# The residual sum r formed by an accumulating transfer on arrival, in place of GpSimd's additions

## The chip, the cores and the metric

The kernel runs on one core of one Trainium2 chip. The metric is the device time of one execution in microseconds (us). TensorE, VectorE, ScalarE, GpSimd and SyncE are called PE, DVE, ACT, POOL and SP in the profile.

## The reference

x has 8 batches of 512 tokens and 2048 features, all in fp32. With W, b the base weight and bias and A, B the low-rank factors that a batch's id selects, the reference computes

```
h    = x @ W.T + b + (x @ A.T) @ B.T
q    = h @ Wq.T
s    = router scores of q against 512 slots (through Wr), plus log_rel
w    = softmax over the 8 best slots of (q . keys / 8 + log_rel)
aux  = (w @ values) @ Wvd.T @ Wvu.T
u    = clip(0.5 * log1p(var(h)) / mean(log1p(var(h))) + 2.5 * sigmoid(gelu(h @ Wu1.T + bu1) @ Wu2.T), 0, 5)
gate = sigmoid(0.5 * clip((u - 0.5) / 1.5, 0, 1) - 1), 0 where under 0.05
out  = x + h + gate * aux
```

The change concerns one sum of the last line, r = x + h. The product gate * aux is added to it at the end.

## The kernel before

Everything lies transposed: a tile is 128 features by 512 tokens in fp32 (256 KB), so a batch is KT = 16 tiles and all eight are 128 tiles. fp32 products are made of three matmuls of a high and a low part.

The first stage (to about 1340 us of the profile) computes h by seven block products for each pair of batches and stores it in DRAM (h_dram). It does not touch r.

The second stage is a loop of STEPS = 128 steps, one tile of h each, batch c = step // 16, k = step % 16. Each engine runs its own copy of the loop in its own fixed order, and semaphores tie them. In a step, SP loads a tile of h into hraw (load_h, a ring of four, four steps ahead); ACT and DVE split it into its high and low part (h_hi, h_lo, two steps ahead, ring h_sp of four); PE does twelve matmuls for Wu1 (u_pass, L1954 to L1956) and two for Wq (L1971, L1972). In the first 16 steps batch 7's query is made too, early, out of the tiles of h that come for r: ACT and DVE split them (h7_hi, h7_lo, ring of two) and PE multiplies them (query7_pass, L1979 and L1980). From step 16 on the work on the batch before (gelu, scores, choice of 8, softmax, transposes, z) is woven into the steps.

r needs a second walk over the tiles, in another order. Its index n runs with the steps. The first NPRE = 32 are batches 7 and 6; ACT stores these sums to r_dram (store_pre), and SP reads them back as r67 (load_last, 512 KB for each k) from step 115 on, for the end. The other 96 are batches 0 to 5: at step 32 + a, PE makes three matmuls of aux for tile a (aux_pass, L2074 to L2076, into one bank), and DVE adds the bank to r's tile and writes o_st (add_out, L1741), which ACT stores (store_out). PE's next aux_pass waits for that addition (out_ready).

For each n, SP loads two tiles in load_r: x into r_x and h into r_h, each a ring of four, two steps ahead. POOL adds them in place into r_h (L891, semaphore r_ready); nothing else is on POOL in these steps but a few memsets. SP's load of x waits for r_ready of n - 4 and its load of h for the store (r_dram, n < 36) or for DVE's add_out (later) of n - 4. What stands behind load_r in SP's queue is the next load_h, and from step 115 load_last.

After step 127 a tail finishes batches 6 and 7 from r67; seven aux banks are copied by ACT into the places of r_x and r_h (evacuated) and added by POOL.

Of the kernel before, what the change touches and what calls it, by code (L numbers as in the profile page):

```python
# [7 lines left out]
KT = D // P  # L8
NB = 8
# [41 lines left out]
def bass_adaln_ffn(  # L51
# [25 lines left out]
    ADD, SUB, MULT = ALU.add, ALU.subtract, ALU.mult  # L77
# [9 lines left out]
    with ctx:  # L87
        def sem(name):
            return ctx.enter_context(nc.semaphore(name))

        def wait(eng, semaphore, value):
            if value > 0:
                eng.wait_ge(semaphore, value)
# [216 lines left out]
        gate_step = sem("gate_step")  # L310
        mstep = sem("mstep")
        ln_ready = sem("ln_ready")
        mean_done = sem("mean_done")
        qb_ready = sem("qb_ready")
        qt_ready = sem("qt_ready")
        qf_ready = sem("qf_ready")
# [13 lines left out]
        zh_ready = sem("zh_ready")  # L330
        zl_ready = sem("zl_ready")
        aux_done = sem("aux_done")
        r_ready = sem("r_ready")
        out_ready = sem("out_ready")
        step_out = [sem(f"step_out{i}") for i in range(4)]
        r67_in = [sem(f"r67_in{i}") for i in range(4)]
# [219 lines left out]
        def evacuated(j):  # L556
            return r_x[:, j, :] if j < 4 else r_h[:, j - 4, :]

        block = ctx.enter_context(nc.Block())


        @block.sync
        def _(sp):
# [104 lines left out]
                sp.dma_start(hraw[:, m % 4, :], h_dram[c, k]).then_inc(hr_in[m % 4], 16)  # L668

            def load_r(n):  # L670
                if n < NPRE:
                    b, o = NB - 1 - n // KT, n % KT
                else:
                    b, o = (n - NPRE) // KT, n % KT
                if n == 0:

                    sp.wait_ge(main_done, TILES - 1)
                    stored(sp, h_index(NPAIR - 1, M5, HT - 1) + 1)
                if n == KT:
                    stored(sp, 4 * HT * NPAIR)  # L680
                wait(sp, r_ready, n - 3)
                sp.dma_start(r_x[:, n % 4, :], x[b, o]).then_inc(rxh_in[n % 4], 16)
                if 4 <= n < NPRE + 4:
                    sp.wait_ge(step_out[n % 4], 16 * (n // 4))
                elif n >= NPRE + 4:
                    sp.wait_ge(out_ready, n - 4 - NPRE + 1)
                sp.dma_start(r_h[:, n % 4, :], h_dram[b, o]).then_inc(rxh_in[n % 4], 16)

            def load_last(k):
                if k < KT - 1:  # L690
# [93 lines left out]
                    sp.wait_ge(a7_out, 16 * TT)  # L784
                sp.dma_start(att[:, t, :], a7_dram[t]).then_inc(a7_in, 16)

            load_r(0)
            load_r(1)
            for step in range(STEPS):
                if step + 4 < STEPS:  # L790
                    load_h(step + 4)
                if step + 2 < STEPS:
                    load_r(step + 2)
                if step >= (NB - 1) * KT + 3:
                    load_last(step - (NB - 1) * KT - 3)
                if step - (NB - 1) * KT in (7, 10, 13):
                    load_a7((step - (NB - 1) * KT - 7) // 3)
# [25 lines left out]
        def _(pool):  # L823
# [61 lines left out]

            pool.wait_ge(qb_ready, 1)
            for n in range(STEPS):
                pool.wait_ge(rxh_in[n % 4], 32 * (n // 4 + 1))
                if n < KT:
                    pool.wait_ge(h7l_ready, n + 1)  # L890
                pool.tensor_tensor(r_h[:, n % 4, :], r_h[:, n % 4, :], r_x[:, n % 4, :], ADD).then_inc(r_ready, 1)  # L891
                if n == KT + 2:
                    pool.wait_ge(h7_used, KT)
                    pool.wait_ge(r_ready, n + 1)
                    pool.memset(qb7[BOT:P, :].bitcast(f32), 1.0).then_inc(qb_ready, 1)
                    pool.wait_ge(qb_ready, 2)
            pool.wait_ge(r_ready, STEPS)
            pool.wait_ge(wgt_ready, len(SEQ) + TT // 2)
            for j in range(KT - BY_DVE):
                o = BY_DVE + j  # L900
# [6 lines left out]
        def _(act):  # L907
# [267 lines left out]
                    .then_inc(gelu_ready, 1)  # L1175

            def h7_hi(n):
                act.wait_ge(rxh_in[n % 4], 32 * (n // 4 + 1))
                wait(act, h7_used, n - 1)
                to_hi(h7_sp[n % 2][:, 0, :], r_h[:, n % 4, :]).then_inc(h7h_ready, 1)  # L1180

            def query_copy(b):
                if b == EARLY:
# [66 lines left out]
                    .then_inc(zh_ready, 1)  # L1250

            def store_pre(n):
                act.wait_ge(r_ready, n + 1)
                act.dma_start(r_dram[n % KT, :, 1 - n // KT, :], r_h[:, n % 4, :]).then_inc(step_out[n % 4], 16)

            def store_out(a):
                act.wait_ge(out_ready, a + 1)
                act.dma_start(out[a // KT, a % KT], o_st[:, a % 4, :]).then_inc(step_out[a % 4], 16)

            def store_step(step):  # L1260
                if step < NPRE:
                    store_pre(step)
                else:
                    store_out(step - NPRE)

            def evacuate(j):
                a = NAUX + BY_DVE + j
                act.wait_ge(aux_done, aux_count(a))
                if j == 0:
                    act.wait_ge(r_ready, STEPS)  # L1270
                    act.wait_ge(out_ready, NAUX)
                act.activation(evacuated(j), aux_place(a)[:], ACT.Copy).then_inc(ev_ready, 1)

            for step in range(STEPS):
                c, k = step // KT, step % KT
                b = c - 1
                if step + 2 < STEPS:
                    h_hi(step + 2)
                if c == 0:
                    h7_hi(k)  # L1280
                if c == 0 and k in (3, 5):
                    split_wvu_hi((k - 3) // 2)
                if c == 0 and k in (5, 7):
                    copy_stats(NB - 2 + (k - 5) // 2)
                if c == 0 and k == 9:
                    act.wait_ge(mstep, 4)
                    act.activation(norm_t[:], var_t[:], ACT.Ln, bias=1.0).then_inc(ln_ready, 1)
                if c >= 1:
                    if k == 0:
                        for m in range(FT):  # L1290
                            gelu(b, m)
                        query_copy(b)
                    if k == 1:
                        query_hi(b)
                    if k == 2:
                        sigmoid_learned(b)
                    if k in MASK_AT:
                        exp_tile(POS[b, MASK_AT[k]])
                    if k == 1 and early_tile(c - 1) is not None:
                        exp_tile(POS[EARLY, early_tile(c - 1)])  # L1300
                    if k == 4 and early_tile(c - 1) is not None:
                        store_a7(early_tile(c - 1))
                    if k == 3:
                        sigmoid_gate(b)
                    if k in TURN_AT:
                        wt_hi(b * TT + TURN_AT[k])
                    if k in Z_AT:
                        z_hi(b, Z_AT[k])
                    if k == 4 and c == 1:
                        query_copy(EARLY)  # L1310
                    if k == 6 and c == 1:
                        query_hi(EARLY)
                if step > 0:
                    store_step(step - 1)

            b, i = NB - 1, (NB - 1) * TT
            for m in range(FT):
                gelu(b, m)
            evacuate(0)
            evacuate(1)  # L1320
            store_step(STEPS - 1)
            sigmoid_learned(b)
            sigmoid_gate(b)
            evacuate(2)
# [15 lines left out]
        def _(dve):  # L1340
# [250 lines left out]

            def h7_lo(n):
                dve.wait_ge(h7h_ready, n + 1)
                lo(h7_sp[n % 2][:, 1, :], r_h[:, n % 4, :], h7_sp[n % 2][:, 0, :]).then_inc(h7l_ready, 1)

            def query_sum(b):
                ps = aux_bank if b == EARLY else q_ps
# [82 lines left out]
                dve.tensor_reduce(rowsum[:], norm_t[:].rearrange("p b t -> p (b t)"), AX.X, ADD).then_inc(mstep, 1)  # L1680

            def mean_of_logs():
                dve.wait_ge(mean_done, 1)
                dve.tensor_scalar(inv_t[:], mean_ps, 1.0 / NTOK, 1e-6, MULT, ADD).then_inc(mstep, 1)
                dve.wait_ge(mstep, 6)
                dve.reciprocal(inv_t[:], inv_t[:]).then_inc(mstep, 1)
                dve.wait_ge(mstep, 7)
                dve.tensor_scalar(norm_t[:], norm_t[:], inv_t[:], 0.5, MULT, MULT).then_inc(mstep, 1)
# [47 lines left out]

            def add_out(a):
                dve.wait_ge(aux_done, a + 1)
                dve.wait_ge(r_ready, NPRE + a + 1)
                dve.wait_ge(step_out[a % 4], 16 * ((NPRE + a) // 4))  # L1740
                dve.tensor_tensor(o_st[:, a % 4, :], aux_bank[:], r_h[:, a % 4, :], ADD).then_inc(out_ready, 1)  # L1741

            def add_last6(o):
                a = NAUX + o
# [88 lines left out]
        def _(pe):  # L1833
# [244 lines left out]
            for step in range(STEPS):  # L2078
                c, k = step // KT, step % KT
                b = c - 1  # L2080
                if c >= 1:
                    if k in TURN_AT:
                        turn_pass(b * TT + TURN_AT[k])
                    if k in Z_AT:
                        z_pass(b, Z_AT[k])
                    if k == 2:
                        learned_pass(b)
                    if k in SCORE_AT:
                        score_pass(POS[b, SCORE_AT[k]])
                    if k == KT - 2 and early_tile(c) is not None:  # L2090
                        score_pass(POS[EARLY, early_tile(c)])
                elif k == 4:
                    stats_pass(NB - 2)
                elif k == 6:
                    stats_pass(NB - 1)
                elif k == 13:
                    pe.wait_ge(mstep, 5)
                    pe.matmul(mean_ps, ones[:], rowsum[:], start=True, stop=True).then_inc(mean_done, 1)
                if 0 <= step - Q7_LAG < KT:
                    query7_pass(step - Q7_LAG)  # L2100
                u_pass(step)
# [81 lines left out]
```

## Time and profile before

| | |
|---|---|
| median of 3 runs | 1915.87 us (1915.84 to 1920.31) |
| profiled execution, its own time | 1916.47 us |
| its span, first to last instruction | 1913.9 us |
| PE busy | 1898.0 us, 99% |
| DVE, ACT, POOL busy | 67%, 37%, 21% |
| DMA traffic | 412 MB, mean 215 GB/s |

The execution's own time is 2.6 us above its span; that part lies outside the trace. A row of a group gives its line, engine, operation, output <- input, shape and count, then busy time in all, mean ns of one, and the idle time of the engine before them with what ended it. Matmul durations overlap: one is listed at 390 ns, but the next starts some 227 ns after it.

### The profile page before, as it was taken

What the parts mean: (1) busy time and instruction counts of PE and PEld (TensorE: products, weight loads), DVE (VectorE), ACT (ScalarE), POOL (GpSimd) and SP (SyncE); (2) the same over time, 40 slices, a digit from 0 to 9 for tenths busy, and PEclk for the clock granted to TensorE, in tenths of its full rate; (3) what the DMA queues carried; (4) which work ended last, traced back from release to release, by engine and by line L of the source; (5) the groups of instructions that cost most, each with busy time, mean ns of one, the idle gap of its engine ahead of it and who ended that gap; (6) DMA issues with size and microseconds to landing.
All of it is one profiled execution on the core that took longest, in us unless ns stands there. A gap on an engine that the chain in (4) does not pass through costs nothing.

```text
span 1913.9 us, 24642 instructions
## 1 busy us (share of the span) xinstructions
PE 1898.0 (99%) x8480; PEld 1550.8 (81%) x8480; DVE 1286.4 (67%) x1686; ACT 714.2 (37%) x1133; POOL 397.4 (21%) x275
## 2 busy tenths in 40 slices
PE   8999999999999999999999999999999999999998
PEld 6888888888888888888888888877888888888887
DVE  5786788565468746447864745777776677677676
ACT  4332344333234333224433333445444234333333
POOL 2210232020023202002310100220443323322332
PEclk9999999999999999999999999999999999999999
DMA  7856877451456745146664425666988777777797
GB/s 279 305 180 216 288 250 230 153 181 60 149 201 232 241 144 179 55 157 216 230 219 146 165 91 192 233 202 226 319 276 286 232 239 243 233 237 247 228 363 295
DMA packets 195633, 412.35 MB, mean 215 GB/s; under 512 B 26740, under 2 KB 28276, under 8 KB 195382
## 3 DMA queue, kind: packets, MB, share of 16 engines
q1 hardware_dynamic: 150006, 321.64, 51.2%
q10 hardware_dynamic: 45504, 89.15, 12.2%
q8 instruction: 68, 1.11, 0.2%
q14 instruction: 55, 0.45, 0.1%
HBM read 313.17 MB, written 97.52 MB: 215 GB/s over the span
## 4 chain that ended last, share of the span: by engine, by line
PE 95%; DVE 3%; ACT 1%; issue 1%; DMA 0%; ACTq 0%; DVEq 0%; SPq 0%
PE bank L1915 21%; PE bank L1916 21%; PE bank L1917 21%; PE bank L1954 6%; PE bank L1955 6%; PE bank L1956 6%; PE bank L1858 2%; PE bank L2074 2%; PE bank L1859 2%; PE bank L2076 1%; PE bank L2075 1%; PE bank L1846 1%; PE bank L1972 1%; PE bank L1971 1%; PE bank L2039 1%
## 5 line engine op out<-in xcount | busy, mean ns | idle before, releaser
L1915 PE MATMUL bank<-xop,wsp 128*128 128x512 f32 x1792 | 701.8, 392 | 6.0 <-DVE wsp L1342 6.0
L1916 PE MATMUL bank<-xop,wsp 128*128 128x512 f32 x1792 | 700.3, 391 | 0.0
L1917 PE MATMUL bank<-xop,wsp 128*128 128x512 f32 x1792 | 699.2, 390 | 0.0
L1915 PEld LDWEIGHTS bank<-xop,wsp 128*128 128x128 f32 x1792 | 337.4, 188 | 85.4 <-DVE wsp L1342 6.4
L1917 PEld LDWEIGHTS bank<-xop,wsp 128*128 128x128 f32 x1792 | 337.1, 188 | 71.8
L1916 PEld LDWEIGHTS bank<-xop,wsp 128*128 128x128 f32 x1792 | 337.6, 188 | 70.6
L909 ACT ACTIVATE wsp<-wraw 128x1024 fp32r<-128x1024 f32 x184 | 195.0, 1060 | 495.7 <-PE bank L1917 487.8
L1342 DVE TENSOR_TENSOR wsp<-wraw,wsp 128x1024 fp32r<-128x1024 f32 x184 | 234.8, 1276 | 154.9 <-ACT wsp L909 154.1
L891 POOL TENSOR_TENSOR r_h<-r_h,r_x 128x512 f32<-128x512 f32 x128 | 175.3, 1370 | 358.3 <-DMA r_h<-h_dram 322.9
L1954 PE MATMUL bank<-h_sp,wu 128*128 128x512 f32 x512 | 200.5, 392 | 1.4 <-DVE stage L1428 1.4
L1955 PE MATMUL bank<-h_sp,wu 128*128 128x512 f32 x512 | 199.8, 390 | 0.0
L1956 PE MATMUL bank<-h_sp,wu 128*128 128x512 f32 x512 | 199.5, 390 | 0.0
L1442 DVE TENSOR_TENSOR sums<-sums,stage 128x1024 f32<-128x1024 f32 x120 | 162.7, 1356 | 0.7 <-ACT stage L994 0.4
L854 POOL TENSOR_TENSOR xraw<-xraw 128x512 f32<-128x512 f32 x32 | 52.2, 1631 | 500.9 <-DMA xraw<-in_x 500.9
L1342 DVE TENSOR_TENSOR xop<-xraw,xop 128x512 fp32r<-128x512 f32 x184 | 153.0, 861 | 3.6 <-ACT xop L909 3.0
L1342 DVE TENSOR_TENSOR h_sp<-hraw,h_sp 128x512 fp32r<-128x512 f32 x128 | 102.8, 803 | 36.4 <-ACT h_sp L909 35.2
L1954 PEld LDWEIGHTS bank<-h_sp,wu 128*128 128x128 f32 x512 | 96.2, 188 | 22.4 <-DVE stage L1428 1.8
L1741 DVE TENSOR_TENSOR o_st<-bank,r_h 128x512 f32<-128x512 f32 x96 | 66.0, 688 | 70.9 <-PE bank L2076 70.6
L1956 PEld LDWEIGHTS bank<-h_sp,wu 128*128 128x128 f32 x512 | 96.1, 188 | 20.7
L1955 PEld LDWEIGHTS bank<-h_sp,wu 128*128 128x128 f32 x512 | 96.2, 188 | 19.6
L909 ACT ACTIVATE xop<-xraw 128x512 fp32r<-128x512 f32 x184 | 107.7, 617 | 5.7 <-DMA xraw<-in_x 5.0
L909 ACT ACTIVATE h_sp<-hraw 128x512 fp32r<-128x512 f32 x128 | 80.1, 627 | 74.3 <-DVE o_st L1741 59.3
(187 smaller groups left out, 1953.7 us busy)
## 6 DMA issues: line engine op xcount, KB each, us to landing
xraw<-in_x SPq DMA_DIRECT2D x248, 256.0 KB, 4.2
wraw<-in_w SPq DMA_DIRECT2D x123, 512.0 KB, 3.8
wraw<-t_dram SPq DMA_DIRECT2D x80, 512.0 KB, 3.6
h_dram<-stage ACTq DMA_DIRECT2D x128, 256.0 KB, 2.7
hraw<-h_dram SPq DMA_DIRECT2D x128, 256.0 KB, 4.1
r_x<-in_x SPq DMA_DIRECT2D x128, 256.0 KB, 4.4
r_h<-h_dram SPq DMA_DIRECT2D x128, 256.0 KB, 3.6
out<-o_st ACTq DMA_DIRECT2D x96, 256.0 KB, 3.9
```

The source lines that it names most:

```text
L854: pool.tensor_tensor(tile, tile, x_raw("b21", p, k), ADD).then_inc(s1_ready, 1)
L891: pool.tensor_tensor(r_h[:, n % 4, :], r_h[:, n % 4, :], r_x[:, n % 4, :], ADD).then_inc(r_ready, 1)
L909: return act.activation(dst, src, ACT.Copy)
L1342: return dve.tensor_tensor(dst, src, hi.bitcast(f32), SUB)
L1442: dve.tensor_tensor(into, into, stage[:, n % NST, :, :], ADD).then_inc(sum_ready, 1)
L1741: dve.tensor_tensor(o_st[:, a % 4, :], aux_bank[:], r_h[:, a % 4, :], ADD).then_inc(out_ready, 1)
L1915: pe.matmul(ps, wsp[:, slot, 0, f], x_hi(i), start=(k == 0), stop=False)
L1916: pe.matmul(ps, wsp[:, slot, 0, f], x_lo(i), start=False, stop=False)
L1917: last = pe.matmul(ps, wsp[:, slot, 1, f], x_hi(i), start=False, stop=(k == HT - 1))
L1954: pe.matmul(u_ps[m][:], wu[k][:, 0, f], h_sp[step % 4][:, 0, :], start=(k == 0), stop=False)
L1955: pe.matmul(u_ps[m][:], wu[k][:, 0, f], h_sp[step % 4][:, 1, :], start=False, stop=False)
L1956: last = pe.matmul(u_ps[m][:], wu[k][:, 1, f], h_sp[step % 4][:, 0, :], start=False, stop=(k == KT - 1))
```

## The change

r is formed by the transfers themselves. SP loads only h, into r_t(n), a place of a ring of eight (the four of r_x and the four of r_h together). When it has landed, and in the first 16 steps also h7_lo has read it, POOL issues a transfer from x in DRAM onto the same tile with accum_op=ADD, so that x is added on arrival. It completes on one of two semaphores r_in (even and odd n), and POOL first waits for the completion of n - 2, so that at most two accumulations are under way. SP's loads run four steps ahead and wait for the user of n - 8. The load order in a step stays load_h, then load_r. ACT stores a pre-sum one step later (store_pre(step - 2) at the end of a step) and waits for r_in of it and for the store of n - 4; store_out stays in its place. add_out waits for r_in of its tile. The semaphore mean_done is replaced by a further count of stats_done. The arithmetic of everything else is unchanged.

```diff
+        def r_t(n):
+            return (r_x if n % 8 < 4 else r_h)[:, n % 4, :]
+        def wait_r(eng, n):
+            eng.wait_ge(r_in[n % 2], 16 * (n // 2 + 1))
...
             def load_r(n):
...
-                wait(sp, r_ready, n - 3)
-                sp.dma_start(r_x[:, n % 4, :], x[b, o]).then_inc(rxh_in[n % 4], 16)
-                if 4 <= n < NPRE + 4:
-                    sp.wait_ge(step_out[n % 4], 16 * (n // 4))
-                elif n >= NPRE + 4:
-                    sp.wait_ge(out_ready, n - 4 - NPRE + 1)
-                sp.dma_start(r_h[:, n % 4, :], h_dram[b, o]).then_inc(rxh_in[n % 4], 16)
+                wait(sp, rxh_in[n % 4], 16 * (n // 4))
+                if n >= 8 and n - 8 < NPRE:
+                    sp.wait_ge(step_out[n % 4], 16 * ((n - 8) // 4 + 1))
+                elif n >= 8:
+                    sp.wait_ge(out_ready, n - 8 - NPRE + 1)
+                sp.dma_start(r_t(n), h_dram[b, o]).then_inc(rxh_in[n % 4], 16)
...
-            load_r(0)
-            load_r(1)
+            for n in range(4):
+                load_r(n)
             for step in range(STEPS):
                 if step + 4 < STEPS:
                     load_h(step + 4)
-                if step + 2 < STEPS:
-                    load_r(step + 2)
+                if step + 4 < STEPS:
+                    load_r(step + 4)
...
             for n in range(STEPS):
-                pool.wait_ge(rxh_in[n % 4], 32 * (n // 4 + 1))
+                b, o = r_source(n)
+                pool.wait_ge(rxh_in[n % 4], 16 * (n // 4 + 1))
                 if n < KT:
                     pool.wait_ge(h7l_ready, n + 1)
-                pool.tensor_tensor(r_h[:, n % 4, :], r_h[:, n % 4, :], r_x[:, n % 4, :], ADD).then_inc(r_ready, 1)
+                if n >= 2:
+                    wait_r(pool, n - 2)
+                pool.dma_start(r_t(n), x[b, o], accum_op=ADD).then_inc(r_in[n % 2], 16)
...
             def store_pre(n):
-                act.wait_ge(r_ready, n + 1)
-                act.dma_start(r_dram[n % KT, :, 1 - n // KT, :], r_h[:, n % 4, :]).then_inc(step_out[n % 4], 16)
+                wait_r(act, n)
+                wait(act, step_out[n % 4], 16 * (n // 4))
+                act.dma_start(r_dram[n % KT, :, 1 - n // KT, :], r_t(n)).then_inc(step_out[n % 4], 16)
...
-                if step > 0:
-                    store_step(step - 1)
+                if 0 <= step - 2 < NPRE:
+                    store_pre(step - 2)
+                if step > NPRE:
+                    store_out(step - 1 - NPRE)
...
             def add_out(a):
                 dve.wait_ge(aux_done, a + 1)
-                dve.wait_ge(r_ready, NPRE + a + 1)
+                wait_r(dve, NPRE + a)
```

## Rows read from the trace of the kernel before

**Rows 1.** The page: busy time by engine, and the chain that ended last.
```profile
PE 1898.0 (99%) x8480; PEld 1550.8 (81%) x8480; DVE 1286.4 (67%) x1686; ACT 714.2 (37%) x1133; POOL 397.4 (21%) x275
...
PE 95%; DVE 3%; ACT 1%; issue 1%; DMA 0%; ACTq 0%; DVEq 0%; SPq 0%
```

**Rows 2.** Busy time by stretch; last columns: granted clock, DMA share, GB/s.
```profile
1340.00:1460.00 120.00, 118.59 (x543) 97.81 (x542) 81.89 (x135) 53.96 (x100) 49.93 (x35) 1.00 0.86 295
1460.00:1840.00 380.00, 378.64 (x1764) 313.66 (x1764) 267.30 (x522) 133.68 (x248) 115.24 (x86) 1.00 0.74 244
1840.00:1880.00 40.00, 40.00 (x195) 33.44 (x194) 24.43 (x46) 11.77 (x22) 10.67 (x8) 1.00 1.00 386
```

**Rows 3.** PE's waits, 1340 to 1880 us: in total, times, longest.
```profile
PE bank L2074 <- DVE o_st L1741: 1.4, 2, 1.0
PE bank L2003 <- DVE qa L1342: 0.8, 1, 0.8
PE bank L1979 <- DVE h_sp L1342: 0.5, 1, 0.5
```

**Rows 4.** Groups by line and shape, 1340 to 1880 us.
```profile
L891 POOL TENSOR_TENSOR r_h<-r_h,r_x 128x512 f32<-128x512 f32 x128 | 175.3, 1370 | 358.3 <-DMA r_h<-h_dram 322.9 <-DVE h_sp L1342 35.4
L1342 DVE TENSOR_TENSOR h_sp<-hraw,h_sp 128x512 fp32r<-128x512 f32 x126 | 101.4, 805 | 36.4 <-ACT h_sp L909 35.2
```

**Rows 5.** Tile acc, durations min/median/max; then timelines of DVE and POOL.
```profile
L1696 DVE TENSOR_SCALAR acc<-gact,wu_sb x8: 476/480/1449, 1396.8 to 1879.3; 128x512 f32<-128x512 f32 x8
...
1396.76 1.45 DVE L1696 TENSOR_SCALAR acc<-gact,wu_sb 128x512 f32<-128x512 f32 x1 [1.23 <-ACT gact L1174]
...
1395.07 4.29 POOL L891 TENSOR_TENSOR r_h<-r_h,r_x 128x512 f32<-128x512 f32 x3 [2.33 <-DVE h_sp L1342]
```

**Rows 6.** Tile r_h: durations ns, first and last start us.
```profile
L1741 DVE TENSOR_TENSOR o_st<-bank,r_h x96: 675/691/693, 1465.1 to 1882.3; 128x512 f32<-128x512 f32 x96
L1254 ACTq DMA_DIRECT2D r_dram<-r_h x32: 326/326/362, 1346.5 to 1459.0; - x32
L909 ACT ACTIVATE h_sp<-r_h x16: 615/632/633, 1342.1 to 1393.6; 128x512 fp32r<-128x512 f32 x16
```

**Rows 7.** DMA issues, 1340 to 1460 us: count, KB, median us to landing.
```profile
r_h<-h_dram SPq DMA_DIRECT2D x33, 256.0 KB, 4.4
hraw<-h_dram SPq DMA_DIRECT2D x33, 256.0 KB, 4.7
r_x<-in_x SPq DMA_DIRECT2D x32, 256.0 KB, 4.8
```

**Rows 8.** DMA issues, 1460 to 1840 us.
```profile
hraw<-h_dram SPq DMA_DIRECT2D x87, 256.0 KB, 4.0
...
r<-r_dram SPq DMA_DIRECT2D x4, 512.0 KB, 5.8
```

**Rows 9.** Timelines of ACT, then DVE: one period of the first sixteen steps.
```profile
1386.30 0.63 ACT L909 ACTIVATE h_sp<-r_h 128x512 fp32r<-128x512 f32 x1 [2.71 <-PE bank L1980]
1386.33 0.33 ACTq L1254 DMA_DIRECT2D r_dram<-r_h  x1
...
1389.94 0.63 ACT L909 ACTIVATE h_sp<-r_h 128x512 fp32r<-128x512 f32 x1 [2.49 <-PE bank L1980]
...
1386.96 0.69 DVE L1342 TENSOR_TENSOR h_sp<-r_h,h_sp 128x512 fp32r<-128x512 f32 x1 [2.57 <-ACT h_sp L909]
```

**Rows 10.** SP's waits, 1340 to 1880 us.
```profile
SPq L687 <- DVE o_st L1741: 268.5, 91, 5.2
SPq L687 <- DMA r_dram<-r_h: 72.5, 25, 5.9
```

**Rows 11.** Two stretches of 6 us, columns as in rows 2.
```profile
1848.00:1854.00 6.00, 6.00 (x34) 5.19 (x33) 4.31 (x9) 0.99 (x2) 1.29 (x1) 1.00 1.05 410
1878.00:1884.00 6.00, 5.69 (x30) 4.58 (x29) 3.94 (x6) 3.83 (x7) 0.00 (x0) 1.00 0.41 136
```

**Rows 12.** DMA issues, 1840 to 1880 us.
```profile
hraw<-h_dram SPq DMA_DIRECT2D x4, 256.0 KB, 8.7
```

More of the change, by code:

```diff
@@ L312, in bass_adaln_ffn @@
         ln_ready = sem("ln_ready")
-        mean_done = sem("mean_done")
         qb_ready = sem("qb_ready")
@@ L332, in bass_adaln_ffn @@
         aux_done = sem("aux_done")
-        r_ready = sem("r_ready")
+        r_in = [sem(f"r_in{i}") for i in range(2)]
         out_ready = sem("out_ready")
@@ L557, in evacuated, with r_source @@
             return r_x[:, j, :] if j < 4 else r_h[:, j - 4, :]
+        def r_t(n):
+            return (r_x if n % 8 < 4 else r_h)[:, n % 4, :]
+        def r_source(n):
+            return (NB - 1 - n // KT, n % KT) if n < NPRE else ((n - NPRE) // KT, n % KT)
+        def wait_r(eng, n):
+            eng.wait_ge(r_in[n % 2], 16 * (n // 2 + 1))
         block = ctx.enter_context(nc.Block())
@@ L670, in load_r @@
             def load_r(n):
[L671 to L674, printed above, removed]
+                b, o = r_source(n)
                 if n == 0:
@@ L887, in _ @@
             for n in range(STEPS):
-                pool.wait_ge(rxh_in[n % 4], 32 * (n // 4 + 1))
+                b, o = r_source(n)
+                pool.wait_ge(rxh_in[n % 4], 16 * (n // 4 + 1))
                 if n < KT:
                     pool.wait_ge(h7l_ready, n + 1)
-                pool.tensor_tensor(r_h[:, n % 4, :], r_h[:, n % 4, :], r_x[:, n % 4, :], ADD).then_inc(r_ready, 1)
+                if n >= 2:
+                    wait_r(pool, n - 2)
+                pool.dma_start(r_t(n), x[b, o], accum_op=ADD).then_inc(r_in[n % 2], 16)
                 if n == KT + 2:
                     pool.wait_ge(h7_used, KT)
-                    pool.wait_ge(r_ready, n + 1)
                     pool.memset(qb7[BOT:P, :].bitcast(f32), 1.0).then_inc(qb_ready, 1)
                     pool.wait_ge(qb_ready, 2)
-            pool.wait_ge(r_ready, STEPS)
+            wait_r(pool, STEPS - 2)
+            wait_r(pool, STEPS - 1)
             pool.wait_ge(wgt_ready, len(SEQ) + TT // 2)
@@ L1177, in h7_hi @@
             def h7_hi(n):
-                act.wait_ge(rxh_in[n % 4], 32 * (n // 4 + 1))
+                act.wait_ge(rxh_in[n % 4], 16 * (n // 4 + 1))
                 wait(act, h7_used, n - 1)
-                to_hi(h7_sp[n % 2][:, 0, :], r_h[:, n % 4, :]).then_inc(h7h_ready, 1)
+                to_hi(h7_sp[n % 2][:, 0, :], r_t(n)).then_inc(h7h_ready, 1)
             def query_copy(b):
@@ L1258, in store_out @@
                 act.dma_start(out[a // KT, a % KT], o_st[:, a % 4, :]).then_inc(step_out[a % 4], 16)
[L1260 to L1264, printed above, removed]
             def evacuate(j):
@@ L1269, in evacuate @@
                 if j == 0:
-                    act.wait_ge(r_ready, STEPS)
+                    wait_r(act, STEPS - 2)
+                    wait_r(act, STEPS - 1)
                     act.wait_ge(out_ready, NAUX)
@@ L1320, in _ @@
             evacuate(1)
-            store_step(STEPS - 1)
+            store_out(NAUX - 1)
             sigmoid_learned(b)
@@ L1593, in h7_lo @@
                 dve.wait_ge(h7h_ready, n + 1)
-                lo(h7_sp[n % 2][:, 1, :], r_h[:, n % 4, :], h7_sp[n % 2][:, 0, :]).then_inc(h7l_ready, 1)
+                lo(h7_sp[n % 2][:, 1, :], r_t(n), h7_sp[n % 2][:, 0, :]).then_inc(h7l_ready, 1)
             def query_sum(b):
@@ L1682, in mean_of_logs @@
             def mean_of_logs():
-                dve.wait_ge(mean_done, 1)
+                dve.wait_ge(stats_done, NB + 1)
                 dve.tensor_scalar(inv_t[:], mean_ps, 1.0 / NTOK, 1e-6, MULT, ADD).then_inc(mstep, 1)
@@ L1738, in add_out @@
                 dve.wait_ge(aux_done, a + 1)
-                dve.wait_ge(r_ready, NPRE + a + 1)
+                wait_r(dve, NPRE + a)
                 dve.wait_ge(step_out[a % 4], 16 * ((NPRE + a) // 4))
-                dve.tensor_tensor(o_st[:, a % 4, :], aux_bank[:], r_h[:, a % 4, :], ADD).then_inc(out_ready, 1)
+                dve.tensor_tensor(o_st[:, a % 4, :], aux_bank[:], r_t(NPRE + a), ADD).then_inc(out_ready, 1)
             def add_last6(o):
@@ L2097, in _ @@
                     pe.wait_ge(mstep, 5)
-                    pe.matmul(mean_ps, ones[:], rowsum[:], start=True, stop=True).then_inc(mean_done, 1)
+                    pe.matmul(mean_ps, ones[:], rowsum[:], start=True, stop=True).then_inc(stats_done, 1)
                 if 0 <= step - Q7_LAG < KT:
```

## Prediction

> **What bounds the kernel now.** I read the page first: PE is busy in 99% of the span and 95% of the chain that ended last is PE's [rows 1]. The change acts only between 1340 and 1880 us, so I read the stretches next. PE lacks 1.4 us of 120 and 1.4 of 380, and nothing of the last 40, at a granted clock of 1.00, which is the level of 2.4 GHz [rows 2]. PE's own waits there name DVE each time, 2.7 us in all [rows 3]; none names POOL or a transfer. DMA is the second resource: a share of 0.86 at 295 GB/s in the first 32 steps, 0.74 at 244 GB/s in the long middle, 1.00 at 386 GB/s at the end [rows 2]. POOL's additions take 175.3 us, but it idles 358.3 us before them [rows 4]: it is no bound. So nearly nothing is to be won, and the question is whether the new transfer takes so much of the DMA engines, or so long, that PE begins to wait.
>
> **What is removed.** 128 additions of 1370 ns on POOL [rows 4]. None lies on PE's chain, so their 175 us are worth nothing by themselves. Their effect on DVE is worth something: while POOL ran three additions in a row from 1395.07, DVE's multiplication of acc took 1.45 us, against a median of 0.48 over its eight occurrences [rows 5]. That slow patch lies just ahead of the place where PE waits 0.8 us for qa, and the 0.5 us for h_sp (L1979) also falls in the first 16 steps, where DVE splits two tiles a step; I count both as won, 1.3 us. Of the 1.4 us for o_st [rows 3], which comes once aux is under way, I count 0.2, because one addition on POOL in 4.39 us seldom meets that chain. Gain 1.5 us; bounds 0 and 2.7 us (all of these waits).
>
> **What is moved.** SP's load of h for r goes four steps ahead, with a ring of eight. Today SP's largest wait there is for the place of r_h, 268.5 us behind DVE's add_out and 72.5 us behind the store [rows 10], and the next load_h stands behind it. With n - 8 in place of n - 4 most of this goes, and SP is then held by load_h's own condition. hraw lands in a median of 4.7 and 4.0 us [rows 7, 8] and no wait of PE names it, so this is cover, not gain: zero. The single load in place of two saves SP some 0.4 us an issue; zero also. store_pre one step later and mean_done folded into stats_done: zero, as the events awaited are the same or older; the price of store_pre's new wait is below.
>
> **What is added.** 128 accumulating transfers that GpSimd issues, of which the trace shows none. Two costs have to be bounded.
>
> First, their share of the DMA engines. An accumulation reads x and the tile and writes the tile. Below, it costs what the load of x costs now (nothing added). Above, I take two plain copies: one more tile, 262 KB, per step. The pace: 32 stores from 1346.5 to 1459.0 us make 3.63 us a step, 96 add_outs from 1465.1 to 1882.3 make 4.39 [rows 6]. One more tile is 72 GB/s early (295 becomes 367) and 60 GB/s in the middle (244 becomes 304). The engines have shown 410 GB/s [rows 11]. So even the upper value fits, at 0.90 and 0.74 of that. I take the upper value. In the last 40 us DMA is full already; about seven accumulations fall there, 1.8 MB, 4.5 us of work at 410 GB/s. It is absorbed: at 1878 to 1884 the share is down to 0.41 [rows 11], and the last tiles of r67 are used in the tail only; hraw lands late there, 8.7 us [rows 12], but is fetched some three steps (13 us) ahead of its split. Zero.
>
> The Trainium skill (Collectives: The Full Stack, The bandwidth ceiling) says that an add in the DMA engine costs no cycles itself but needs two source reads, and gives a ratio of 1.93. By it the added share would be 0.93 of a tile, 67 GB/s in place of my 72, and the sum is the same; no row here shows an accumulation.
>
> Second, their latency L, from issue to landing. Only two may be under way, so one is finished every L/2. For L below: x's plain landing of 4.8 us [rows 7] and ACT's issue of 0.33 [rows 6], 5.1 us. Above: two plain landings after each other, 4.8 + 4.4 [rows 7], and a GpSimd issue as long as the addition it replaces, 1.37 [rows 4]: 10.6 us. Nearest is the transfer that reads as much as an accumulation does, 512 KB, with 5.8 us [rows 8]. Scaled to the fuller first 32 steps by hraw's 4.7 to 4.0 it is 6.8, with an issue of 0.33 to 1.37 it is 7.1 to 8.2 us early and 6.1 to 7.2 later. I take 7.1, at the low end, as the reads of x and of the tile go on side by side in 16 engines.
>
> What L costs PE early: batch 7's tile is split by ACT at 1386.30, DVE has read it at 1387.65 and then the accumulation may start. ACT's new store stands two periods of 3.64 us later, at 1393.58 [rows 9], so 5.9 us of L are hidden. ACT idles 2.5 us a step there [rows 9], and it splits for PE two steps ahead, of which some 5 us are left after the two splits: PE waits only when the store is 7.5 us late. At L = 7.1 the pair's pace is 3.55 us, the store is 1.2 us late, and ACT's idle time takes it. But lag adds up: the first 16 steps take only 3.43 us each (15 intervals from 1342.1 to 1393.6 [rows 6]), and from the first store to the last it is 112.5 us. The last pre-sum lands 31 L/2 + L = 16.5 L after the first may start, and PE's limit is 112.5 + 5.9 + 7.5 = 125.9 us: L = 7.6 us. Later the limit is 2 x 4.39 = 8.8 us, with a lead of four steps on top. At 7.1 both hold: zero.
>
> Queued behind the waits: on ACT the splits of the next step; on POOL only the next accumulation; on SP (h for r waits for the store of n - 8) load_h. All three are covered as long as L is under the limit.
>
> **Sum.** 1.5 us less. Against the profiled execution 1916.47 becomes 1915.0; it lay 0.6 us above the median of 1915.87, so the median becomes 1914.4 us. 0.3% is 5.7 us, about what a measurement of this kernel can tell from no change, so this is "same".
>
> **Rivals.** (a) *Two at a time is too few.* From L = 7.6 us on PE waits for ACT's splits, and from 8.1 the net loss passes 5.7 us. At L = 9: early 16.5 x 9 - 125.9 = 23 us, later (4.5 - 4.39) x 96 = 10 us, in all +33, less 1.5: 1947 us. At the bound of 10.6 it is 49 + 87 us and 2050. For it: L's upper half; landings stretch to 8.7 us when the engines are full [rows 12]. Against: 410 GB/s is well above 367. It is the slower case that I hold likeliest, and store_pre's wait is its place.
>
> The Trainium skill (SBUF - State Buffer, SBUF: two separate sides) has a rule against this change: a transfer issued by GpSimd can stall because GpSimd writes its descriptors through a port that DVE's two-port operations lock. This would lengthen L; the trace shows only that POOL and DVE slow each other [rows 5], and no GpSimd transfer. In this kernel such operations are few and short (0.48 us), so it enters as part of rival (a).
>
> (b) *The DMA engines become the bound.* If an accumulation costs four plain copies in place of one, a step moves seven tiles, 1.83 MB, 4.48 us at 410 GB/s: +0.85 x 32 + 0.09 x 96 = 36 us, less 1.5: 1950 us. It decides from 2.6 copies on early ((410 - 295) x 3.63 / 262 = 1.6 tiles of room) and from 3.8 later. DMA's share would stand at 1.00 over the whole loop.
>
> (c) *PE gains more than its waits.* A gain over 5.7 us would need more than the 2.7 us of waits, so a change in the tail (1880 to 1913.9), where POOL's seven additions stay. 1909 us. Nothing speaks for it.
>
> (d) *It does not matter at all*, because the waits of [rows 3] are DVE's own chain and stay: 1915.9 us. It lies inside the likeliest case.
>
> **Chances.** Likeliest with (d), within 0.3%: 0.59. (a) 0.24, (b) 0.13, (c) 0.04. So faster 0.04, same 0.59, slower 0.37. The likeliest's own range is 1912 to 1921. For 8 in 10 the low end takes the gain's bound (1913.2) and a little for run spread, 1912; the high end takes (a) up to L = 9 (1947) and leaves out what lies above, most of (b) too: 1947.
>
> **What the profile after would show.** DVE's waits on PE's list fall from 2.7 us towards 1.2, and the 1.45 us multiplication returns to 0.48; if not, the gain is wrong. DMA's share in the first 32 steps is 0.95 to 1.00 and in the middle 0.8 to 0.95; if it stays at 0.74 an accumulation is cheap, if it is 1.00 everywhere (b) holds. Issue to landing of the accumulation under 7.6 us: if over 8.1, ACT's splits wait for r and PE for h_sp, and (a) holds. SP's wait behind add_out nearly vanishes.

## The result, and the profile after

The changed kernel takes 1920.59 us in the median of 20 runs, the kernel before 1917.86 us in 20 runs beside them: a ratio of 1.0013, 95% interval 1.0007 to 1.0019. It is slower by 0.13%, or 2.7 us. The size is inside the forecast's "same" (0.3%) and inside its range, but the sign is wrong: 1.5 us less was forecast, and the interval excludes no change. The profiled execution took 1921.71 us with a span of 1919.7 us, 5.8 us above the span before, a high draw, as that of before was a low one of its own runs.

The page of the changed kernel, as [rows 1]:

```profile
span 1919.7 us, 24772 instructions
...
PE 1900.7 (99%) x8480; PEld 1552.4 (81%) x8480; DVE 1253.1 (65%) x1686; ACT 713.8 (37%) x1133; POOL 333.5 (17%) x275
...
PE 92%; DMA 3%; DVE 2%; ACT 1%; issue 1%; SPq 0%; ACTq 0%; DVEq 0%; POOLq 0%
```

DMA has appeared on the chain that ended last, with 3%. Busy time by stretch, columns as in [rows 2]:

```profile
1340.00:1460.00 120.00, 115.36 (x511) 94.49 (x510) 68.24 (x130) 49.13 (x94) 29.92 (x35) 0.97 1.02 282
1460.00:1840.00 380.00, 379.02 (x1771) 314.40 (x1770) 249.00 (x517) 136.08 (x251) 76.07 (x88) 1.00 0.93 246
1840.00:1880.00 40.00, 40.00 (x191) 33.31 (x190) 25.59 (x52) 10.42 (x20) 6.05 (x7) 1.00 1.07 350
```

All that was lost is lost in the first 32 steps: PE lacks 4.6 us of 120 there, against 1.4 before, and the mean granted clock is 0.97. Later PE is as busy as before or busier. PE's waits around and after the join of the two stages, the larger ones, as [rows 3]:

```profile
PE bank L1960 <- ACT gact L1182: 3.6, 1, 3.6
PE bank L1960 <- DVE stage L1434: 1.1, 1, 1.1
PE bank L2080 <- DVE o_st L1747: 0.9, 1, 0.9
PE bank L1985 <- DVE h_sp L1348: 0.6, 1, 0.6
PE bank L1874 <- ACT stats L1008: 0.5, 1, 0.5
```

The wait for stage is not new: it lies in the first step of the second stage, and in the kernel before it is 1.4 us and ends at 1338.95, just ahead of where [rows 3] begin. The wait for qa is gone and that for o_st shorter (0.9 in place of 1.4 us), as forecast in kind; that for h_sp stays. New is a wait of 0.5 us for ACT's copy of the statistics, at 1360.49, and one of 3.6 us for the gelu of batch 0, at the first matmul of step 16. ACT's own timeline says why it was late:

```profile
1392.04 0.33 ACTq L1263 DMA_DIRECT2D r_dram<-r_x  x1
1392.47 0.63 ACT L917 ACTIVATE h_sp<-hraw 128x512 fp32r<-128x512 f32 x1 [4.32 <-DMA r_x<-in_x]
...
1394.55 0.33 ACTq L1263 DMA_DIRECT2D r_dram<-r_h  x1
...
1398.34 0.33 ACTq L1263 DMA_DIRECT2D r_dram<-r_h  x1
1398.77 0.63 ACT L917 ACTIVATE h_sp<-hraw 128x512 fp32r<-128x512 f32 x1 [2.64 <-DMA r_h<-in_x]
1399.42 1.28 ACT L1182 ACT_TABLE_LOAD   x1
1400.71 0.69 ACT L1182 ACTIVATE gact<-bank,bu_sb 128x512 f32<-128x512 f32 x1
```

The store at 1398.34 is that of n = 13, which stands in ACT's queue at the end of step 15. It was held until x had been added to that tile. Only then came the next split, the load of gelu's table and the gelu. PE had started its last matmul of step 15 at 1397.57, and up to there it had lost 0.5 us, the wait for the statistics: the first step begins 0.3 us and this one ends 0.9 us later than before. The chain that ended last goes through the accumulations here:

```profile
1378.39 6.06 DMA r_x<-in_x
1384.51 0.49 issue
1385.00 7.02 DMA r_x<-in_x
1392.09 0.49 issue
1392.58 5.75 DMA r_h<-in_x
1398.34 0.33 ACTq L1263
```

Three accumulations after one another in one of the two lanes (even n and odd n), each let in by the landing of n - 2 and 0.5 us later under way. It was so, within a microsecond, in both lanes from n = 5 to n = 15. GpSimd's issues of n = 3 and n = 13:

```profile
1355.84 0.86 POOL L899 DMA_DIRECT2D r_x<-in_x  x1 [1.52 <-DVE h_sp L1348]
...
1392.58 0.86 POOL L899 DMA_DIRECT2D r_h<-in_x  x1 [4.33 <-DMA r_x<-in_x]
```

Ten tiles in 36.7 us are 3.67 us per tile, 7.35 us a round. PE's own steps from 3 to 13 take 36.8 us in the kernel before, so r kept pace but could not catch up what it was late from the start on. The other part of the loss is the clock. Four-microsecond stretches, columns as above:

```profile
1396.00:1400.00 4.00, 1.96 (x9) 1.30 (x7) 1.51 (x3) 1.35 (x3) 0.86 (x1) 1.00 1.10 276
1400.00:1404.00 4.00, 2.45 (x6) 2.00 (x7) 2.37 (x5) 3.96 (x7) 0.86 (x1) 0.60 1.05 309
1404.00:1408.00 4.00, 4.00 (x12) 3.10 (x11) 3.68 (x6) 1.42 (x3) 0.86 (x1) 0.55 1.07 313
```

The granted clock fell to the level of 1.2 GHz at 1400.8, while PE still waited, and stayed there until 1407.6: 14 matmuls started 0.43 us apart in place of 0.23, another 2.8 us. With the waits of 3.6 and 0.5 that makes 6.9 us; less what went of the others (0.8 for qa, 0.5 for o_st, 0.3 for stage) it is 5.3 us. The spans differ by 5.8 us, and the second stage began 0.3 us later (its first matmul at 1336.38 in place of 1336.04), so 0.2 us are left.

DMA in the first 120 us of the loop, queues and issues, as [rows 7]:

```profile
q1 hardware_dynamic: 9478, 17.26, 42.0%
q0 software_dynamic: 4738, 8.64, 42.0%
q10 hardware_dynamic: 4320, 7.87, 17.6%
...
hraw<-h_dram SPq DMA_DIRECT2D x32, 256.0 KB, 6.0
r_x<-in_x POOLq DMA_DIRECT2D x18, 256.0 KB, 6.1
...
r_h<-in_x POOLq DMA_DIRECT2D x16, 256.0 KB, 6.5
```

q0 is GpSimd's. It takes the same share as SP's q1 with half of the packets of the same mean size: 0.420 x 16 x 120 us / 4738 = 170 ns a packet against 85.

### The profile page after: what moved, and what is told of

It is laid out like the page before. It is cut to its first block, busy times and chain, and to the rows that moved or that the text cites. A ratio compares the mean times of both kernels' runs of the same rounds, so it can differ in the third digit from the quotient of the medians.

```text
span 1919.7 us, 24772 instructions
## 1 busy us (share of the span) xinstructions
PE 1900.7 (99%) x8480; PEld 1552.4 (81%) x8480; DVE 1253.1 (65%) x1686; ACT 713.8 (37%) x1133; POOL 333.5 (17%) x275
## 4 chain that ended last, share of the span: by engine, by line
PE 92%; DMA 3%; DVE 2%; ACT 1%; issue 1%; SPq 0%; ACTq 0%; DVEq 0%; POOLq 0%
PE bank L1921 20%; PE bank L1922 20%; PE bank L1923 20%; PE bank L1960 5%; PE bank L1961 5%; PE bank L1962 5%; PE bank L1864 2%; PE bank L2080 2%; PE bank L1865 2%; PE bank L2082 1%; PE bank L2081 1%; PE bank L1852 1%; PE bank L2045 1%; PE bank L1978 1%; PE bank L1977 1%; DMA r_x<-in_x 1%
## 5 line engine op out<-in xcount | busy, mean ns | idle before, releaser
L1448 DVE TENSOR_TENSOR sums<-sums,stage 128x1024 f32<-128x1024 f32 x120 | 158.7, 1322 | 0.7 <-ACT stage L1002 0.4
L1348 DVE TENSOR_TENSOR h_sp<-hraw,h_sp 128x512 fp32r<-128x512 f32 x128 | 88.2, 689 | 67.9 <-ACT h_sp L917 66.2
L853 POOL TENSOR_TENSOR xraw<-xraw,v_t 128x512 f32<-128x512 f32 x32 | 54.6, 1717 | 243.6 <-DMA xraw<-in_x 243.6
L1002 ACT ACTIVATE stage<-stage 128x512 f32<-128x512 f32 x128 | 79.3, 619 | 40.4 <-DVE stage L1434 37.6
```

What stands on the lines that cost most here:

```text
L853: pool.tensor_tensor(tile, tile, v_t[:, k, :], ADD).then_inc(s2_ready, 1)
L1002: act.activation(stage[:, n % NST, 1, :], stage[:, n % NST, 0, :], ACT.Square).then_inc(sq_ready, 1)
L1348: return dve.tensor_tensor(dst, src, hi.bitcast(f32), SUB)
L1448: dve.tensor_tensor(into, into, stage[:, n % NST, :, :], ADD).then_inc(sum_ready, 1)
```

## The experiments

Each was timed against the kernel before on the same chip. Theory A is ACT's place in the queue; theory B, that the DMA engines are full.

**The changed kernel again.**

> The changed kernel again, unaltered, as the base of this set. Theory A (ACT's place): in the first 16 steps two accumulations at a time finish one per 3.5 us or slower against 3.43 us a step, ACT waits for r_in in store_pre, comes late to the four gelus of step 16, PE waits some 3 to 4 us for them and then runs some 6 us at the lower clock: +2 to +5 us over before, with the wait for gelu in the trace in most executions. Theory B (the DMA engines are full in the first 32 steps): the same time, but the lost time would be spread, without one single wait.

1920.88 us, ratio 1.0010 (1.0001 to 1.0018). Its profile has the same single long wait, 3.6 us for gact, and the same pace of 3.67 us per tile from n = 3 to 13. The clock was at 1.2 GHz for half as long behind it, 3.4 us (1404.1 to 1407.5), which is 8 matmuls and 1.6 us. The wait of theory A repeats; the price of the clock varies.

**Four accumulations under way.**

```diff
-            eng.wait_ge(r_in[n % 2], 16 * (n // 2 + 1))
+            eng.wait_ge(r_in[n % 4], 16 * (n // 4 + 1))
...
-                if n >= 2:
-                    wait_r(pool, n - 2)
+                if n >= 4:
+                    wait_r(pool, n - 4)
```

> Four accumulations may be under way in place of two; nothing else changes (two freed semaphores come from the r67 loads sharing v_in). Theory A: the pace of two at a time is gone, ACT is in time for gelu, PE's wait for gelu falls to 0 and the clock stays 1.00: 3 to 6 us less than the changed kernel, level with before or 1 us under it. Theory B: the engines were full with two; four under way only lengthen each landing (from 6 to 10 us or more), ACT waits as long and the time stays at +2 to +5 us.

1916.07 us, ratio 0.9991 (0.9982 to 1.0000): 2.2 per thousand (4.2 us) less than the changed kernel's 1.0013, as A says; against its repeat in this set it is 1.9 per thousand. But the wait for gelu did not go to zero. PE's wait and the landings from 1340 to 1460 us:

```profile
PE bank L1959 <- ACT gact L1181: 2.1, 1, 2.1
...
hraw<-h_dram SPq DMA_DIRECT2D x33, 256.0 KB, 7.0
r_x<-in_x POOLq DMA_DIRECT2D x19, 256.0 KB, 7.3
```

With more under way each lands later (7.3 against 6.1 us) and so does h itself. ACT's last wait ahead of the gelus is for such a load of h, with the store of n = 13 issued at 1395.05 inside it:

```profile
1395.59 0.63 ACT L916 ACTIVATE h_sp<-hraw 128x512 fp32r<-128x512 f32 x1 [2.22 <-DMA hraw<-h_dram]
```

B holds for that part: the engines are full (a share of 1.03), and ACT stays near the edge.

**The stores issued by GpSimd.**

```diff
+                if 0 <= n - 2 < NPRE:
+                    wait(pool, r_st[(n - 2) % 4], 16 * ((n - 2) // 4))
+                    pool.dma_start(r_dram[(n - 2) % KT, :, 1 - (n - 2) // KT, :], r_t(n - 2)).then_inc(r_st[(n - 2) % 4], 16)
...
-                if 0 <= step - 2 < NPRE:
-                    store_pre(step - 2)
```

> The 32 stores of the pre-sums are issued by GpSimd, after its own wait for r_in of n - 2, so that ACT waits for no accumulation; two at a time stay, and GpSimd gets a second issue per step. Theory A: PE's wait for gelu is gone although the accumulations are as slow, the time is level with before (+-1 us). Theory B: the time stays at +2 to +5 us, as the DMA work is the same.

1924.22 us, ratio 1.0032 (1.0021 to 1.0043): slower, which neither theory gave. The wait for gelu shrank to 0.9 us as A says, but a new one came:

```profile
PE bank L2076 <- DVE o_st L1743: 6.5, 2, 5.7
```

It is at the first aux products. PE's second ones wait for DVE's first add_out, and DVE stood still before that:

```profile
1471.41 0.69 DVE L1743 TENSOR_TENSOR o_st<-bank,r_x 128x512 f32<-128x512 f32 x1 [6.56 <-DMA r_x<-in_x]
```

ACT no longer waits for r, so nothing slowed the loop when r fell behind: PE began the first aux products 6.4 us earlier than in the changed kernel (1462.12 against 1468.51), while the accumulation of their tile, n = 32, was issued 8.4 us later (1463.52 against 1455.13). The first reader paid, and 6.8 us at 1.2 GHz followed. GpSimd's queue had a second wait and a second issue for each tile here; how much of the delay is theirs was not taken apart. This is the prediction's rival (a), two at a time being too few, at a different place.

**The stores of n = 12 and 13 after the gelus.**

```diff
                     if k == 0:
                         for m in range(FT):
                             gelu(b, m)
+                        if c == 1:
+                            for n in (12, 13):
+                                store_pre(n)
...
-                if 0 <= step - 2 < NPRE:
+                if 0 <= step - 2 < NPRE and step - 2 not in (12, 13):
                     store_pre(step - 2)
```

> ACT makes the stores of n = 12 and 13 after the gelus of step 16; nothing else moves. Theory A: the lateness that reaches the gelus is that of store 11 (n = 12 and 13 no longer count), so PE's wait shrinks from 3.6 to about 0 to 1 us and the clock holds: 3 to 5 us less than the changed kernel. Theory B: no change.

1916.48 us, ratio 0.9991 (0.9983 to 1.0000). PE has no wait for gact. ACT's timeline:

```profile
1395.31 0.62 ACT L917 ACTIVATE h_sp<-hraw 128x512 fp32r<-128x512 f32 x1
1395.94 1.28 ACT L1182 ACT_TABLE_LOAD   x1
1397.24 0.69 ACT L1182 ACTIVATE gact<-bank,bu_sb 128x512 f32<-128x512 f32 x1
```

The gelu starts 3.5 us earlier than in the changed kernel, with the DMA share as high as there (1.02 and 1.05 in the two 60 us from 1340, against 1.00 and 1.03). That is A alone.

**The transfer without the addition.**

```diff
-                pool.dma_start(r_t(n), x[b, o], accum_op=ADD).then_inc(r_in[n % 2], 16)
+                pool.dma_start(r_t(n), x[b, o]).then_inc(r_in[n % 2], 16)
```

> GpSimd issues the same transfers without the addition (accum_op left out, so r is x alone and the sum x + h is left out). Both theories so far charge the accumulation itself: if it costs the DMA engines two copies, the time of GpSimd's queue falls from 10.7% of 16 engines to about 5.5%, the share in the first 32 steps from 1.02 to about 0.87, the landing from 6.3 to about 5 us, PE's wait for gelu goes, and the time is 1914 to 1917 us. If the cost lies in GpSimd's issuing and not in the addition, the landing stays above 6 us and the time stays at +2 to +5 us over before.

1914.88 us, ratio 0.9978 (0.9969 to 0.9987): the fast end of what was expected. GpSimd's queue and issues from 1340 to 1460 us:

```profile
q0 software_dynamic: 2880, 9.44, 25.5%
...
r_x<-in_x POOLq DMA_DIRECT2D x20, 256.0 KB, 4.8
...
r_h<-in_x POOLq DMA_DIRECT2D x17, 256.0 KB, 5.3
```

2.7% of the engines for each MB against 4.9% with the addition, and 4.8 to 5.3 us to landing against 6.1 to 6.5. So the cost is in the addition, not in who issues. Against the changed kernel it is 1.0013 - 0.9978, 3.5 per thousand, 6.7 us; the two ratios come from different sets, and by their intervals this is 3.5 +- 1.1.

**One accumulation at a time.**

```diff
-                if n >= 2:
-                    wait_r(pool, n - 2)
+                if n >= 1:
+                    wait_r(pool, n - 1)
```

> Only one accumulation may be under way. Theory A (their pace): one is finished every L + 0.5 us, about 5.5 to 6.8 us against steps of 3.5 and 4.4 us, PE then waits for r in the whole loop: + (6.3 - 3.5) x 32 + (5.8 - 4.4) x 96 = 90 + 130 us, with L shorter as the engines are emptier, so +100 to +220 us. Theory B (the engines' work is the limit, not the count under way): the share falls a little and the time grows by under 20 us.

2069.61 us, ratio 1.079 (1.0769 to 1.0811), +151 us. GpSimd's issues run from 1347.1 to 2025.3 us for 128 tiles, 5.3 us each: the landing is 4.6 us in the median, as the share is lower (0.86 in the first 60 us, 0.78 in the middle), and the rest is GpSimd's. With the loop's pace before, 3.63 and 4.39 us a step, (5.34 - 3.63) x 32 + (5.34 - 4.39) x 96 is 146 us, near the 151. Theory B's 20 us is far off; with one under way the time from issue to landing sets the pace, as A says.

**The kernel before with POOL's additions cut to 8 columns.**

```diff
-                pool.tensor_tensor(r_h[:, n % 4, :], r_h[:, n % 4, :], r_x[:, n % 4, :], ADD).then_inc(r_ready, 1)
+                pool.tensor_tensor(r_h[:, n % 4, 0:8], r_h[:, n % 4, 0:8], r_x[:, n % 4, 0:8], ADD).then_inc(r_ready, 1)
```

> The kernel before with POOL's additions cut to 8 of 512 columns (the rest of the sum is left out), loads and order unchanged. It prices what the removal of POOL's work is worth by itself: the prediction's gain of 1.5 us, with PE's waits for qa and h_sp (0.8 and 0.5 us) gone and DVE's 1.45 us multiplication back at 0.48. If those waits are DVE's own chain, they stay and the time is unchanged within 0.5 us.

1914.75 us, ratio 0.9977 (0.9968 to 0.9987): 4.4 us, three times the forecast gain, by the interval 2.5 to 6.1 us. PE's waits from 1340 to 1880 us, and DVE's split, which is faster (groups by line, as [rows 4]):

```profile
PE bank L1954 <- DVE stage L1428: 1.4, 1, 1.4
PE bank L2074 <- DVE o_st L1741: 0.9, 1, 0.9
PE bank L1979 <- DVE h_sp L1342: 0.6, 1, 0.6
```
```profile
L1342 DVE TENSOR_TENSOR h_sp<-hraw,h_sp 128x512 fp32r<-128x512 f32 x126 | 86.7, 688 | 42.3 <-ACT h_sp L909 40.7
```

The wait for qa is gone and that for o_st is 0.9 in place of 1.4 us; that for h_sp, which the forecast had counted as won, stays. The wait for stage is as long in the kernel before (1.4 us) and only fell into the window here. So the waits of the two profiles differ by 1.2 us, not by 4.4.

**Where that gain lies.** The additions were cut for n < 32 only, and for the other 96 only.

```diff
+                w = S if n >= 32 else 8
-                pool.tensor_tensor(r_h[:, n % 4, :], r_h[:, n % 4, :], r_x[:, n % 4, :], ADD).then_inc(r_ready, 1)
+                pool.tensor_tensor(r_h[:, n % 4, 0:w], r_h[:, n % 4, 0:w], r_x[:, n % 4, 0:w], ADD).then_inc(r_ready, 1)
```

> The kernel before with POOL's additions cut to 8 of 512 columns for n < 32 only (that part of the sum is left out), the other 96 whole. It places the 4 us that cutting all additions brought. If POOL holds DVE up where DVE has two tiles a step to split and the batch boundary at 1400 us follows (PE's wait for qa there), this brings nearly all of it: 3 to 4 us less than before. If the loss is spread over the loop, it brings a quarter: 1 us.

> The complement: additions whole for n < 32, cut to 8 of 512 columns for the other 96 (that part of the sum is left out). By the first view it brings 0 to 1 us, by the second about 3 us. If neither this nor the other half brings anything, the 4 us were not additive, and a single late event (whichever comes) explains them.

1916.22 us, 0.9995 (0.9986 to 1.0004), and 1916.83 us, 0.9997 (0.9988 to 1.0006). Neither half has the gain of the whole, and neither can be told from no change. The halves add up to 0.8 thousandths against 2.3; with three intervals of about 0.9 on two chips that difference may also be scatter. In the first, PE's wait for qa is gone, in the second it is there with 0.9 us. Where the rest of the 4.4 us lies is not settled.

**Two further profiles of the kernel before.**

> The kernel before, unaltered, for a second profile. Its executions lie between 1915.3 and 1921 us, and the profiled one was at 1916.5, the low end. In a slower execution the trace should show the wait that makes the difference: expected is a longer wait of PE for DVE at a batch boundary (qa or o_st), with POOL's additions on top of DVE's operations, and a stretch at a lower granted clock behind it.

> As the look before: a third profile of the kernel before, to see whether the same wait varies from execution to execution.

They took 1916.52 and 1918.29 us. The first has the waits of [rows 3] again (o_st 0.9), the second more of them. Its PE waits from 1340 to 1880 us, in part:

```profile
PE bank L1954 <- DVE stage L1428: 1.8, 1, 1.8
PE bank L2074 <- DVE o_st L1741: 1.2, 2, 0.9
PE bank L2003 <- DVE qa L1342: 1.1, 2, 0.8
PE bank L2031 <- DVE att L1648: 0.6, 1, 0.6
```

The wait for att and a second one for qa do not stand in [rows 3]. So the profiled execution of before, at 1916.47 us, showed less of DVE's lateness than this one near the median. From the first matmul of u_pass to the start of its last group the three profiles of before took 542.6, 541.8 and 544.9 us, that with the light additions 541.1: 0.7 to 3.8 us less. No single long wait was seen.

**Four under way and the two stores moved.** The two edits above together.

> Four accumulations under way and the stores of n = 12 and 13 behind the gelus of step 16, both together. If the wait for gelu was all that the change cost, this is at the level of the deferred stores alone (1916.5 us, 1 to 2 us under before), with no wait for gelu and none for r; if a full DMA queue costs something of its own, it is slower than that by 1 to 3 us.

1917.74 us, ratio 0.9996 (0.9987 to 1.0006): not better than either edit alone. Its profile has no wait for gact, but the DMA share is 1.04 and 1.07 in the two stretches of 60 us from 1340. That a full queue costs something of its own fits, but the intervals overlap with those of the single edits, and it stays open.

**Only the store of n = 13 moved, and the two stores once more.**

> Only the store of n = 13 goes behind the gelus of step 16. In the profile of the changed kernel ACT was released from the store of n = 12 at 1394.5 us and from that of n = 13 at 1398.3, while PE's last matmul of step 15 ended near 1397. If that one store is what counts, this equals the two-store version: 1916.5 us, 3 to 5 us under the changed kernel. If earlier lateness counts as well, it stands between them, at 1918 us.

> The stores of n = 12 and 13 behind the gelus, as e4_defer, timed once more: a ratio to before of 0.9985 to 0.9995, so that the two together are under before by more than their intervals. If the first measurement was luck, it is 1.0000 or more.

1916.73 us, 0.9992 (0.9983 to 1.0001), and 1916.02 us, 0.9989 (0.9980 to 0.9998). The first has no wait for gact in its profile:

```profile
1396.15 1.28 ACT L1182 ACT_TABLE_LOAD   x1
1397.44 2.43 ACT L1182 ACTIVATE gact<-bank,bu_sb 128x512 f32<-128x512 f32 x4
1399.58 0.33 ACTq L1263 DMA_DIRECT2D r_dram<-r_h  x1
```

The store of n = 13 now goes at 1399.58, past the four gelus. One store of 32, moved behind the four gelus, turns the change from 1.0013 into 0.9992. The version with two stores moved was measured twice, at 0.9991 and 0.9989. Of the versions that do the whole computation none is faster (four under way is level with it, 0.9991), and it is 0.1% under before. Its intervals end at 1.0000 and 0.9998, so it beats the kernel before by little, if at all, and the changed kernel clearly. In the profile of the second run PE waits for gact again, but for 0.5 us.

## Why the prediction was wrong

**What bounds the kernel: right.** PE's 99% stayed, and the time moved by 0.13%.

**The gain: right in kind, mis-sized.** The step "Gain 1.5 us; bounds 0 and 2.7 us" measured 4.4 us (0.9977) where POOL's additions were cut alone. The 2.7 us of waits in [rows 3], those of one profiled execution, were taken as a bound, and even the low end of the interval, 2.5 us, nearly reaches it. That execution had fewer waits than another of the same kernel, which is part of the fault; where the rest of the 4.4 us lies stays open. Of the 1.3 us counted as won in the first 32 steps, qa's 0.8 went and h_sp's 0.5 did not; o_st gave 0.5 for the 0.2 counted. The multiplication of acc is back at 0.48 us, as forecast.

**The cost of an accumulation in the engines: the upper bound was right.** Two plain copies were taken, and 170 against 85 ns a packet were measured, two times as much. The ratio of 1.93 that the Trainium skill (Collectives: The Full Stack, The bandwidth ceiling) gives for an add with its two source reads agrees within 4%. But the conclusion "even the upper value fits, at 0.90 of that" said nothing of latency: hraw landed in 6.0 us in place of 4.7, and the share read 1.02. GB/s, which counts the tile once, did not show it: 282 against 295.

**The latency: right.** L = 7.1 us was taken. Landing of 6.1 to 6.5 plus 0.5 us from release to issue makes 6.6 to 7.0, and n = 13 landed 52.8 us after n = 0 was issued (1345.5 to 1398.3), which by the prediction's own sum, 7.5 L, is L = 7.04. The step to hold it against was misread: 3.43 us is the spacing of ACT's splits, of which the first come in a burst, while PE's steps 3 to 13 take 3.68 on average. The error lay on the careful side. The rule against the change (the Trainium skill, SBUF - State Buffer, SBUF: two separate sides), that DVE's two-port operations starve GpSimd's descriptors, does not show in this kernel: plain transfers from GpSimd landed as SP's do (4.8 to 5.3 against 4.8 to 5.4 us in that run), with DVE as busy (72 us of the 120, against 68).

**What L costs PE: wrong, and this is the step that failed.** "ACT idles 2.5 us a step there, and it splits for PE two steps ahead ... PE waits only when the store is 7.5 us late", and with it "Queued behind the waits: on ACT the splits of the next step". It held up to step 15, but for 0.5 us of wait for the statistics. In step 16 what is queued behind store_pre is the four gelus, for which PE waits at its first matmul of the step: there, no instruction of ACT runs ahead. By the prediction's reckoning the store of n = 13 was due at 1394.9 (the end of DVE's read of the tile, 1388.95, plus 5.9 us). It was let go at 1398.34, 3.5 us late, where the prediction's own numbers for L = 7.1 give some 2.8 (1.2, and 13 tiles of 0.12 us). So lateness of this order was in the forecast, and the slack was not 7.5 us but none: 3.5 us late cost PE a wait of 3.6. Moving that one store shows it: the wait goes, and the time falls by 2.1 per thousand, 4.0 us.

**The clock: missing.** No term stood for what a wait does afterwards. The 3.6 us cost 2.8 us more in one profile and 1.6 in the other.

**The rivals.** (a) named the mechanism, two at a time and ACT's wait in store_pre, and put its threshold at L = 7.6 us. With the gelus as victim an estimate is 6.6: the landing of n = 13 would have had to come 3.6 us earlier, 49.2 us after the first issue, and 49.2 / 7.5 is 6.6. (b) did not come (two copies, not four, and a share of 0.93 in the middle), nor did (c). (d) is refuted: the wait for qa went with POOL's additions, and the interval of that run lies wholly under 1.

**The balance,** in thousandths of the time, each a measured ratio to before: without POOL's additions -2.3; the same with GpSimd's plain transfers -2.2, so that no cost of the issuing shows; with the addition in the engines and one or two stores moved -0.8 to -1.1; as changed +1.3. So the addition costs 3.5, of which 2.1 to 2.4 are the wait for gelu with its clock. What is left, 1.1 to 1.4, goes with the fuller engines, but this was not taken apart, and with intervals of 0.9 on each ratio it is barely clear of noise.

## What to carry to other kernels

Before a wait is put into an in-order queue, look at every step for what stands behind it, not at the usual step: slack from running ahead is worth nothing at the few places where an instruction answers the bottleneck engine at once (here the gelus, and for 0.5 us the statistics). A store that nobody is waiting for belongs behind such an instruction. And the waits of one fast profile are no bound on a gain: look at a second one, nearer to the median.

## What the runs showed of the hardware

- A packet of an accumulating transfer occupied a DMA engine for 170 ns against 85 for a load. The bytes of the profile do not count its second read (8.64 MB for 34 tiles of 0.26); the share does.
- GpSimd's issue of one 128-partition accumulating transfer takes 862 ns in the median (0.54 us without the addition), and starts some 0.5 us after the wait that held it. With one at a time this made 5.3 us per tile for a landing of 4.6.
- A wait of 3.6 us in PE went with 6.8 us at the level of 1.2 GHz in one profile (mean granted clock 0.60 and 0.55 in two stretches of 4 us) and with 3.4 us in another of the same kernel. Four under way, with a wait of 2.1 us, had a mean of 0.98 over the 60 us from 1400.
- 128 additions of 1.37 us on GpSimd, never on the chain, cut to 8 columns made the kernel 4.4 us (2.5 to 6.1) faster. DVE's split took 805 ns beside them and 688 without; that the gain comes by way of DVE is argued from this, not shown.
